# Banded attention of layer 0 on 32-row float32 tiles; in layer 1 the first maxima from such tiles, and maxima 26 units ahead

## The reference, cut to what matters

```python
x = x + _L0_attn_ref(_layernorm(x, axis=-1), L0_attn_Wq, L0_attn_Wk, L0_attn_Wv, L0_attn_Wo)
...
x = x + _L1_attn_ref(_layernorm(x, axis=-1), L1_attn_Wq, L1_attn_bq, L1_attn_Wk, L1_attn_bk, L1_attn_Wv, L1_attn_bv, L1_attn_Wo, L1_attn_bo)
...
    scores = jnp.einsum('bhqd,bhkd->bhqk', q, k) * scale
    attn = jax.nn.softmax(scores, axis=-1)
    out = jnp.einsum('bhqk,bhkd->bhqd', attn, v)
```

## Time and profile before

| what | value |
|---|---|
| median of 3 runs | 2615.79 us (2614.08 to 2620.44) |
| the profiled execution | 2614.69 us, span 2613.0 us |
| mean granted TensorE clock | 0.901 of full speed |
| PE, DVE, ACT, POOL busy | 80%, 65%, 46%, 23% of the span |
| layer 0's self-attention | 22.67 to 281.45 us |
| layer 1's self-attention | 666.94 to 989.82 us |

### The profile page before, as it was taken

The page is one execution under the profiler, slowest core; times in us unless marked ns, Lnnn a source line. Parts: engine busy times, 40 slices in busy tenths (PEclk is TensorE's granted clock), DMA queues, the critical chain, the costliest instruction groups (busy, mean ns, idle before and its releaser), DMA issues. The chain is left out here.

```text
span 2613.0 us, 28449 instructions
## 1 busy us (share of the span) xinstructions
PE 2086.1 (80%) x10279; PEld 1314.2 (50%) x10309; DVE 1706.7 (65%) x2551; ACT 1189.9 (46%) x1889; POOL 588.5 (23%) x346
## 2 busy tenths in 40 slices
PE   5789889695689997969875788888788989283895
PEld 3456557584323324857732444444475654161574
DVE  5555455423677755732177999999965766858675
ACT  2334422110266673511046899999943236412340
POOL 3331122120242212012100675565301210000100
PEclk8889999698799998969988899999989989696896
DMA  6554220343655500034310000000031000000001
GB/s 127 87 87 46 71 97 1 107 155 117 107 73 73 65 1 22 1 110 147 119 59 38 0 1 1 1 1 1 33 102 37 1 0 1 0 8 22 1 1 39
DMA packets 108550, 127.88 MB, mean 49 GB/s; under 512 B 15591, under 2 KB 99444, under 8 KB 107381
## 3 DMA queue, kind: packets, MB, share of 16 engines
q1 hardware_dynamic: 100118, 113.45, 18.8%
q0 software_dynamic: 2880, 7.48, 0.8%
q10 hardware_dynamic: 5408, 5.07, 0.6%
HBM read 92.29 MB, written 33.29 MB: 48 GB/s over the span
## 5 line engine op out<-in xcount | busy, mean ns | idle before, releaser
L3360 DVE TENSOR_TENSOR_SCAN l2s_h<-l2w_aw 128x2048 f32<-128x2048 f32 x64 | 290.1, 4533 | 5.0 <-ACT l2s_rs L3483 5.0
L3288 PE MATMUL l2s_big<-g_xn,g_ident 128*128 128x512 f32 x512 | 258.5, 607 | 11.4 <-ACT g_xn L3476 6.3
L3447 POOL TENSOR_SCALAR l2w_aw<-l2w_aw 128x2048 f32<-128x2048 f32 x64 | 212.2, 3316 | 141.5 <-DVE l2w_aw L3352 136.3
L591 DVE TENSOR_REDUCE l1at_nm<-l1at_s 128x1 f32<-128x512 f32 x256 | 161.9, 683 | 67.6 <-PE l1at_s L441 66.6
L3280 PE MATMUL l2s_c_ps<-g_ident,l2s_h 128*128 128x128 f32 x1024 | 148.9, 279 | 55.8 <-ACT g_xn L3476 36.8
L3280 PEld LDWEIGHTS l2s_c_ps<-g_ident,l2s_h 128*128 128x128 f32 x1024 | 117.2, 142 | 146.5 <-issue 86.9
L691 ACT ACTIVATE g_xn<-l1at_s 128x512 f32<-128x512 f32 x256 | 143.6, 598 | 84.5 <-PE l1at_s L465 83.9
L3476 ACT ACTIVATE g_xn<-l2s_c_ps,l2s_ct 128x512 f32<-128x512 f32 x256 | 162.5, 686 | 16.0 <-PE l2s_c_ps L3280 15.6
L591 DVE TENSOR_REDUCE l0at_nm<-l0at_s 128x2 f32<-128x384 f32 x128 | 69.7, 556 | 90.0 <-PE l0at_s L441 88.9
L3469 ACT ACTIVATE l2w_aw<-l2s_dt,l2w_A 128x2048 f32<-128x2048 f32 x64 | 128.2, 2004 | 0.0
L3288 PEld LDWEIGHTS l2s_big<-g_xn,g_ident 128*128 128x128 f32 x512 | 82.0, 190 | 81.7 <-ACT g_xn L3476 59.1
(11 more groups left out here) (873 smaller groups left out, 4811.9 us busy)
## 6 DMA issues: line engine op xcount, KB each, us to landing
l1f_w<-in_L_ffn_w_dram SPq DMA_DIRECT2D x16, 1024.0 KB, 6.5
l0f_w<-L_ffn_experts_inter_dram SPq DMA_DIRECT2D x7, 1024.0 KB, 5.3
l0f_w<-n_L_ffn_experts_out_dram SPq DMA_DIRECT2D x7, 1024.0 KB, 9.7
l0at_qs<-l0at_parts SPq DMA_DIRECT2D x18, 256.0 KB, 9.1
l0at_ks<-l0at_parts SPq DMA_DIRECT2D x18, 256.0 KB, 17.9
l1at_qs<-l1at_parts SPq DMA_DIRECT2D x18, 256.0 KB, 9.1
l1at_ks<-l1at_parts SPq DMA_DIRECT2D x18, 256.0 KB, 20.8
expert_rows<-g_zeros SPq DMA_DIRECT2D x1, 4096.0 KB, 12.8
```

The lines of the kernel that those rows point to most:

```text
L591: V.tensor_reduce(nm[:, s % 2, qts[0]:qts[-1] + 1, r], s1[:, u % 3, 0:len(qts) * KEYS].rearrange("p (q k) -> p q k", k=KEYS), AX, ALU.max, ...
L3288: nc.tensor.matmul(acc[:, tb, :], ident[:], hCT[:, tb, :], start=n == 0, stop=n == NST - 1).then_inc(acc_done, 1)
L3360: V.tensor_tensor_scan(out=h_all[:, i % 2].rearrange("p c t -> p (c t)"), data0=dA[:, i % 2].rearrange("p c t -> p (c t)"), data1=wd[:, i ...
L3447: nc.gpsimd.tensor_scalar(wd[:, i % 3], wd[:, i % 3], 10.0, -10.0, ALU.min, ALU.max).then_inc(clipped, 1)
```

## The change

**Layer 0** gets a function of its own, `banded_attention`. q and k don't travel through DRAM any more. ACT evacuates each projected half twice in float32 into `qz` and `kz`, once for the even and once for the odd heads, with the other heads' rows multiplied by zero (`own`), and with a one in a free row of `kz` (`top`). Four heads of the same parity then lie on 32 partitions each. `max_scores` takes 64 queries by 128 keys at a time from such a 32-row slice, four matmuls in a unit (two halves of 64 output columns, two query tiles); the band is added by DVE in the same instruction that takes the maximum (`tensor_tensor_reduce`). The maxima are turned in float32 by PE and added into the free row of `qz` by DVE (`place_maxima`). `prob_scores` takes two matmuls with 128 output columns and 192 (or 128) query columns from the 32-row slices, without a mask. After ACT's exponential POOL sets what lies outside of the band to zero (`cut`, two chained `affine_select`s in a unit), and `weigh` waits for that. A unit's maxima come `LEAD` = 14 units ahead of its probabilities.

**Layer 1** keeps the stacks for all probabilities and for the maxima from group 2 on. The maxima of groups 0 and 1 come from `qz` and `kz`, 32-row float32 slices made by DVE (`head_tiles`). Maxima run 26 units ahead, projections and values stand at places of the lead-in (`EARLY`), `full` and the parts have two buffers, and each batch's stacks are waited for in two halves.

The diff, cut to its core (the first four pieces are layer 1's):

```diff
     RING = 8
-    AT_NM, AT_TURN, AT_BACK, AT_Y, AT_LOAD = (1, 4, 6, 7, (3, 5)) if window else (3, 7, 11, 14, (8, 12))
+    AT_MAX, AT_HEADS, AT_BACK, AT_OUT = 8, 7, 11, 14
+    AT_LOAD = (3, 11)
+    LEAD = 2 * NU + 2 - AT_MAX
+    FIRST = 2
+    EARLY = {1: ("qk", 0, 1), 3: ("qk", 0, KC + 1), 5: ("v", 0, 0), 7: ("v", 0, 1),
+             9: ("qk", 1, 0), 11: ("qk", 1, KC), 13: ("qk", 1, 1), 15: ("qk", 1, KC + 1)}
...
+                def max_scores(m):
+                    s, r, q = max_unit(m)
+                    b, g = s // GROUPS, s % GROUPS
+                    if m == 0:
+                        pe.wait_ge(tiles_made, 2)
+                    if m % NU == 0 and s >= FIRST and g % 2 == 0:
+                        pe.wait_ge(loaded[b][g // 2], NL)
+                    if m >= 3:
+                        pe.wait_ge(s1_free, m - 2)
+                    h, at = g * GH + r, slice(q * P, (q + 1) * P)
+                    if s < FIRST:
+                        rows = slice(2 * HD * (h // 2), 2 * HD * (h // 2 + 1))
+                        left, right = qz[rows, h % 2, at], kz[rows, h % 2, :]
+                    else:
+                        left, right = qs[0:KROWS, b % 2, h, at], ks[0:KROWS, b % 2, h, :]
+                    nc.tensor.matmul(s1[:, m % 3, :], left, right, start=True, stop=True).then_inc(s1_ready, 1)
...
+                project(0, 0)
+                project(0, KC)
+                pe.wait_ge(cleared, 1)
+                for u in range(-LEAD, TOTAL):
+                    s, i = u // NU, u % NU
+                    b, g = s // GROUPS, s % GROUPS
+                    if u >= 0:
+                        prob_scores(u)
+                    if u + LEAD < TOTAL:
+                        max_scores(u + LEAD)
+                    if u + LEAD in EARLY:
+                        kind, n, j = EARLY[u + LEAD]
+                        project(n, j) if kind == "qk" else values(n, j)
+                    if u >= 0 and weighed_at(u) is not None:
+                        weigh(weighed_at(u))
+                    if i == AT_MAX and 0 <= s + 1 < NG:
+                        turn_maxima(s + 1)
...
+                def head_tiles():
+                    dve.wait_ge(own_made, 1)
+                    for n, to in enumerate((qz, kz)):
+                        bank, at, number = qk_at[0, n * KC]
+                        dve.wait_ge(bank.free, number)
+                        for e in range(2):
+                            ins = V.tensor_scalar(to[:, e, :], full[:, 0, n * KC, :], own[:, e:e + 1], None, ALU.mult)
+                        ins.then_inc(tiles_made, 1)
...
+def banded_attention(nc, name, c, wts):
...
+    BAND = 64
+    SPAN = P + BAND
+    NU = GH * QT // 2
+    NW = NU // GH
+    TOTAL = NG * NU
+    UNIT = 2 * SPAN
+    RING = xn.shape[1] * DM // UNIT
+    LAG = 4
+    AT_MAX, AT_HEADS = 4, 6
+    AT_BACK, AT_OUT = (1, 0), (1, 2)
+    AT_QK, AT_V = ((0, 0, 1), (2, 0, 1)), (3, 0, 1)
+    LEAD = 2 * NU + 2 - AT_MAX
+    EARLY = {3: ("qk", 1), 5: ("qk", KC + 1), 7: ("v", 0), 9: ("v", 1)}
...
+    def heads_of(o, e):
+        return [2 * GH * o + 2 * r + e for r in range(GH)]
+
+    def max_unit(m):
+        s, i = m // NU, m % NU
+        return s, (i + 2 - LEAD) % GH, (2 * (i // GH), 2 * (i // GH) + 1)
+
+    def prob_unit(u):
+        s, i = u // NU, u % NU
+        return s, i % GH, (2 * (i // GH), 2 * (i // GH) + 1)
...
+                def max_scores(m):
+                    s, r, qts = max_unit(m)
+                    b, o, e = place_of(s)
+                    if m % NU == 0 and e == 0:
+                        for j in (o, KC + o):
+                            pe.wait_ge(qk_at[b, j][0].free, qk_at[b, j][2])
+                    if m >= 3:
+                        pe.wait_ge(s1_free, m - 2)
+                    rows = slice(HP * r, HP * (r + 1))
+                    for v, q in enumerate(qts):
+                        for half in range(2):
+                            q0 = q * P + half * BAND
+                            k0 = max(q0 - BAND, 0)
+                            ins = nc.tensor.matmul(s1[half * BAND:(half + 1) * BAND, m % 3, v * P:(v + 1) * P], qz[rows, b % 2, o, e, q0:q0 + BAND],
+                                                   kz[rows, b % 2, o, e, k0:k0 + P], start=True, stop=True)
+                    ins.then_inc(s1_ready, 1)
...
+                def prob_scores(u):
+                    s, r, kts = prob_unit(u)
+                    b, o, e = place_of(s)
+                    if u % NU == 0:
+                        pe.wait_ge(A.free, nm_at[s])
+                    if u >= 2:
+                        pe.wait_ge(exp_done, u - 1)
+                    rows = slice(HP * r, HP * (r + 1))
+                    for v, kt in enumerate(kts):
+                        q0, n = columns(kt)
+                        ins = nc.tensor.matmul(s2[:, u % 2, v * SPAN:v * SPAN + n], kz[rows, b % 2, o, e, kt * P:(kt + 1) * P],
+                                               qz[rows, b % 2, o, e, q0:q0 + n], start=True, stop=True)
+                    ins.then_inc(s2_ready, 1)
...
+                def weigh(w):
+                    s = w // NW
+                    b, o, e = place_of(s)
+                    pe.wait_ge(cut_done, (w + 1) * GH)
...
+                    for v, kt in enumerate(prob_unit(w * GH)[2]):
+                        q0, n = columns(kt)
+                        for r, h in enumerate(heads_of(o, e)):
+                            ins = nc.tensor.matmul(o_ps[HP * r:HP * r + HP, q0:q0 + n], vb[:, b % 2, kt, h, :],
+                                                   pT[:, (w * GH + r) % RING, v * SPAN:v * SPAN + n], start=kt == 0, stop=kt == QT - 1,
+                                                   skip_group_check=True)
+                    ins.then_inc(pv_done, 1)
...
+                def maximum(m):
+                    s, r, qts = max_unit(m)
+                    e = place_of(s)[2]
+                    col = HP * r + HD * (1 - e)
+                    dve.wait_ge(s1_ready, m + 1)
+                    for v, q in enumerate(qts):
+                        to = nmx[:, s % 2, q, col:col + 1]
+                        ins = V.tensor_tensor_reduce(masked[:, m % 3, v], s1[:, m % 3, v * P:(v + 1) * P], mask[:, 1 if q else 0, :], -1.0, 3e38,
+                                                     ALU.add, ALU.min, to)
+                    ins.then_inc(s1_free, 1)
+
+                def place_maxima(s):
+                    b, o, e = place_of(s)
+                    dve.wait_ge(A.ready, nm_at[s])
+                    V.tensor_tensor(qz[:, b % 2, o, e, :], qz[:, b % 2, o, e, :], m_ps[:, 0, :], ALU.add).then_inc(A.free, 1)
...
+                def evacuate(b, j):
+                    bank, at, number = qk_at[b, j]
+                    n, o = j // KC, j % KC
...
+                        act.wait_ge(s2_ready, ((b - 2) * GROUPS + 2 * o + 2) * NU)
+                    for e in range(2):
+                        bias = top[:, 1 - e:2 - e] if n else 0.0
+                        ins = E.activation((qz, kz)[n][:, b % 2, o, e, :], m_ps[:, at, :], ACT.Identity, bias=bias, scale=own[:, n, e:e + 1])
...
+                def cut(u):
+                    pool.wait_ge(exp_done, u + 1)
+                    slot = pT[:, u % RING].rearrange("p (v t) -> p v t", t=SPAN)
+                    near, far = slot[:, :, 0:P], slot[:, :, SPAN - P:SPAN]
+                    Chain(pool, cut_step, u).step(G.affine_select(out=near, in_=near, compare_op=ALU.is_ge, fill=0.0, base=0, pattern=[[0, 2], [1, P]],
+                                                                  channel_multiplier=-1))
+                    G.affine_select(out=far, in_=far, compare_op=ALU.is_ge, fill=0.0, base=0, pattern=[[0, 2], [-1, P]],
+                                    channel_multiplier=1).then_inc(cut_done, 1)
...
-            self_attention(nc, "l0at", c, of("L0_attn_"), given=False, window=True)
+            banded_attention(nc, "l0at", c, of("L0_attn_"))
```

More of the change, by code:

```diff
@@ L346, in self_attention @@
         wo = S.sb("wo", [P, KC, DM])
[L347 to L365, removed]
@@ L367, in self_attention @@
+        with nc.allow_non_contiguous_dma(reason="bias vectors by feature"):
+            prepare(nc, name + "t", c, loads, [])
         qs, ks = (S.sb(n, [P, 2, HEADS, SEQ], BF16) for n in ("qs", "ks"))
+        qz, kz = (S.sb(n, [P, 2, SEQ]) for n in ("qz", "kz"))
+        blocks, own = S.sb("blocks", [P, 2 * GH]), S.sb("own", [P, 2])
         vb = S.sb("vb", [P, 2, QT, HEADS, HP])
-        full = S.sb("full", [P, 2 * KC, SEQ])
-        part = [S.sb(n, [P, 2 * KC, SEQ], BF16) for n in ("hi", "mid", "lo")]
+        full = S.sb("full", [P, 2, 2 * KC, SEQ])
@@ L371, in self_attention @@
+        part = [S.sb(n, [P, 2, 2 * KC, SEQ], BF16) for n in ("hi", "mid", "lo")]
         identb = S.sb("identb", [P, P], BF16)
         pick = S.sb("pick", [P, GH, SEQ], BF16)
-        mask = S.sb("mask", [P, 2, 2, SPAN], BF16) if window else None
```

(34 more changed lines are left out.)

609 lines of the change are left out of this document (406 added, 203 removed).

## The result

| | us |
|---|---|
| changed kernel, median of 4 runs | 2841.16 (2828.98 to 2853.02) |
| kernel before, beside it, median of 3 runs | 2615.79 (2614.08 to 2620.44) |
| ratio, 95% interval | 1.0857 (1.0796 to 1.0918) |
| layer 0's attention in the profiles | 450.6 after (22.39 to 472.94), 258.8 before |
| layer 1's attention | 351.7 after (860.01 to 1211.67), 322.9 before |

What follows compares the result with a forecast made beforehand. PE was taken to bound layer 0, with no waiting in its steady part. 2614.7 us, plus 41.6 for layer 0, less 7 for layer 1, plus 1.1 from profiled run to median, gave 2650; 8-in-10 range 2540 to 2685.

Steps and rivals of the forecast that it cites:

- the rival with the lower one: Layer 0: PE gets its lower 1.2 GHz clock for 32-row work, scores cost 131 us more, 2780 us; chance 0.03.
- The sum at the full clock: Layer 0's attention: PE work of 288.4 us plus about 12 us idle makes 300.4 us, against 258.8 before.
- Scores: Layer 0 on PE: probabilities 76.0 us, maxima 55.3 and shape changes 51.2, together 182.5 us.
- two changes of shape: Layer 0 on PE: each unit switches tile shape and back, 0.20 us lost each time, 51.2 us for 256.
- the idle time: Layer 0: PE idles about 8 us at the start and 4 at the end.
- The faster rival: Layer 0: tiles of different widths on different rows run side by side, 0.54 us a unit, 2550 us; chance 0.32.
- POOL and DVE: Layer 0: POOL's select 0.41 us, DVE's maximum two steps of 0.285 plus at most 0.159 us, all hidden behind PE.
- The POOL rival: Layer 0: POOL's selects become the bound at four times their price alone, 2.5 us a unit, 2697 us; chance 0.06.
- forecast -7: Layer 1's start: earlier maxima and probabilities save 7.8 + 2.6 - 3.5 us, so -7 us, bounds -2 and -15.
- the seventh unit's maximum waits for the second half: Layer 1's start: PE stops there for batch 0's stack until about 714 us, probabilities queued behind.
- about 700: Layer 1's lead-in: float32 maxima, six projections and batch 0's values fill PE to about 700 us.
- 6 x 0.43: Layer 1's start: PE is six probability units ahead when the stack arrives, worth 2.6 us.

## Why the prediction was wrong, point by point

- **The step that failed: the clock.** Every PE term of layer 0 was priced at the full clock, and the rival with the lower one had a chance of 0.03, "For it: 0.81 to 0.90 here, but those are stretches with waits". PE hardly waits now and has 0.57. The runs on 128 rows show up to 173 us for it. That rival's time, 2780, was too low as well: it doubled the scores alone, but all of PE's work in the stretch slows down, projections, weighing and transposes too.
- **The sum at the full clock** was 300.4 us for layer 0; the run on 128 rows measured 277.4. Scores: 182.5 forecast. Where the changed kernel's clock is 1.00, its units take 1.42 and 1.32 us, 1.37 in the mean, 176 us for 128; the mean work is 1.03 us as priced, so two changes of shape cost 0.35 us, not 0.40. On 128 rows the mean is 1.34, 171 us. The other 11 us lie in the idle time (12 forecast, 6.0 measured on 128 rows) and in the small terms, which no run tells apart. Even at the full clock, one tile at a time would lose 19 us to before. So the direction was right, but what the forecast had as its cause makes some 20 of the 225 us; that the change is slower by far has another one.
- **The faster rival**, tiles on different rows side by side although their shapes differ, is wrong: the maxima start where the probabilities end. But its mechanism holds for equal shapes, which the changed kernel's order uses only in the lead-in.
- **POOL and DVE** were priced about right: 0.41 us a select, and 0.288 + 0.083 us for each of DVE's two steps of a unit's maximum. Neither holds PE up. (The POOL rival's "four times its price alone" is 3.3 times by the forecast's own line, 0.35 us for 192 elements; the selects took 0.41 us for 256, so nothing hangs on it.)
- **Layer 1**, forecast -7, measured +28.8. The stack was no longer what PE waited for: "the seventh unit's maximum waits for the second half" didn't happen, PE gets there at 935.8, 76 us behind the layer's start, and has no DMA wait. Three terms were missing or too small. The float32 tiles are made by DVE first, so the first maximum comes 13.0 us behind the start. The 26 maxima of the lead-in lie one after the other (the two between projections share their rows), 0.96 us each and more where the clock falls, so "about 700", 33 us behind the start, became 60. And the six float32 maxima between the first probabilities were left out of "6 x 0.43"; with them it is 6 x 2.54 us. The turning of the maxima, 7 us, wasn't looked at.

## What to carry to other kernels

In these runs a matmul on 32 rows cost as much PE time as one on 128 at the same clock, and where such matmuls filled the time one by one, a unit cost nearly twice that (2.41 for 1.32 us), because the granted clock fell to its lower level though PE hardly ever idled: price it at both levels, and look at the clock of each stretch ahead of its waits. Equal tiles on different row groups cost next to nothing extra if they directly follow each other (two units 1.47 us, one 1.42), so order units by shape, two and two; here that was worth 200 us. What replaces a wait must be shorter than the wait: 26 float32 maxima in the lead-in took longer than the stacks were late.

## What the runs showed of the hardware

- The clock follows the rows at work, not only the busy time: PE busy for 418.6 of 422 us at 0.57; the same columns on 128 rows, 1.00; pairs of 32-row tiles, 0.82 to 0.89. The Trainium skill's page TensorE: Matmul & The Clock Gate, Part 1, says that the clock depends on how busy PE has been. By that rule alone layer 0 would have kept the upper level; the measurement decides.
- With such work the clock differs between executions of the same code: the layer 0 in pairs unit by unit took 239.0 and 243.9 us in two profiles, with 0.89 and 0.87, the one in turn 255.0 and 242.5, with 0.82 and 0.87, and the changed kernel's four runs spread over 24 us, those of the kernel before beside the experiments over 3 to 14.
